# One output scale spread over all partitions by DMA through DRAM in place of TensorE, with reordered loads, shifts, banks and a split last tile

## What is computed

```python
mod = (silu(c) @ wmod).reshape(4, 6, 1, 512)
sa, ca, ga, sb, cb, gb = (mod[:, i] for i in range(6))
ga = sign(ga) * max(abs(ga), 0.25)              # gb likewise
h = layernorm(x) * (1 + ca) + sa
x = x + ga * attention(h, Wqkv, bqkv, Wo, bo)   # one head of 128
h = layernorm(x) * (1 + cb) + sb
x = x + gb * (h @ W_up.T + lora_of_top1_expert(h))
```

## Time and profile before

| | before |
|---|---|
| three runs, us | 184.07, 186.6, 189.16 (median 186.6) |
| the profiled execution, us | 184.51 |
| its span, first to last instruction, us | 182.8 |
| granted TensorE clock over the span | 1.000 (the level of 2.4 GHz) |
| busy share: PE, DVE, ACT, POOL | 93%, 76%, 49%, 44% |

### The profile page before, as it was taken

The page is one execution under the profiler, slowest core; times in us unless marked ns, Lnnn a source line. Parts: engine busy times, 40 slices in busy tenths (PEclk is TensorE's granted clock), DMA queues, the critical chain, the costliest instruction groups (busy, mean ns, idle before and its releaser), DMA issues.

```text
span 182.8 us, 2810 instructions
## 1 busy us (share of the span) xinstructions
PE 170.1 (93%) x911; PEld 133.6 (73%) x911; DVE 139.8 (76%) x350; ACT 90.3 (49%) x170; POOL 81.0 (44%) x109
## 2 busy tenths in 40 slices
PE   6778999999999959998999999999999999999990
PEld 6654756978678738786888787868887878768870
DVE  1837859997969999869997919699288294988964
ACT  3356145964268874176438552713396512484100
POOL 3464200279335984008769830018695000362650
PEclk9999999999999999999999999999999999999999
DMA  4999995930051014440023741001140000001414
GB/s 155 381 385 387 390 383 98 375 120 11 0 166 69 2 26 105 102 170 6 32 83 136 190 107 31 0 0 57 61 152 24 0 2 0 0 0 61 172 43 186
DMA packets 13758, 21.32 MB, mean 117 GB/s; under 512 B 3324, under 2 KB 3840, under 8 KB 13744
## 3 DMA queue, kind: packets, MB, share of 16 engines
q1 hardware_dynamic: 13744, 21.15, 34.3%
HBM read 14.83 MB, written 4.21 MB: 104 GB/s over the span
## 4 chain that ended last, share of the span: by engine, by line
PE 65%; DVE 18%; ACT 6%; DMA 4%; issue 4%; SPq 1%; POOL 0%; DVEq 0%; ACTq 0%; POOLq 0%
PE bank L391 43%; DMA stage<-in_L_wmod_dram 4%; PE bank L405 3%; DVE h1lo L1137 3%; PE bank L515 3%; DVE xs L1215 2%; DVE stats L1222 2%; PE bank L542 2%; DVE row_max L1189 2%; ACT xn_p L830 2%; DVE f_gb L1280 2%; DVE h2lo L1153 1%; DVE xn L1148 1%; PE bank L494 1%; PE bank L500 1%
## 5 line engine op out<-in xcount | busy, mean ns | idle before, releaser
L391 PE MATMUL bank<-wup_lo,h2hi 128*128 128x512 f32 x64 | 26.8, 418 | 1.3 <-DVE f_gb L1280 0.9
L1466 POOL TENSOR_TENSOR rstd<-var_eps,neg_half 128x1 f32<-128x1 f32 x16 | 8.8, 553 | 41.4 <-DVE var_eps L1226 41.4
L869 ACT ACTIVATE xn_p<-xs,shift,rstd 128x512 f32<-128x512 f32 x16 | 13.1, 817 | 25.9 <-POOL shift L1469 25.9
L391 PE MATMUL bank<-wup_hi,h2hi 128*128 128x512 f32 x64 | 25.3, 395 | 0.0
L391 PE MATMUL bank<-wup_hi,h2lo 128*128 128x512 f32 x64 | 25.2, 394 | 0.0
L1481 POOL TENSOR_TENSOR xs<-xs,f_gb 128x512 f32<-128x512 f32 x14 | 17.9, 1294 | 7.7 <-DVE f_gb L1280 7.7
L391 PE MATMUL bank<-h1lo,wqkv_hi 128*128 128x512 f32 x48 | 19.7, 410 | 0.8 <-DVE modT_ca L1057 0.8
L1458 POOL TENSOR_TENSOR xs<-xs,gabo 128x512 f32<-128x512 f32 x16 | 20.2, 1293 | 0.1
L391 PE MATMUL bank<-h1hi,wqkv_hi 128*128 128x512 f32 x48 | 19.0, 395 | 0.0
L391 PE MATMUL bank<-h1hi,wqkv_lo 128*128 128x512 f32 x48 | 18.9, 394 | 0.0
L391 PEld LDWEIGHTS bank<-wup_lo,h2hi 128*128 128x128 f32 x64 | 12.0, 188 | 4.5 <-DVE f_gb L1280 1.8
(11 more groups left out here) (181 smaller groups left out, 414.5 us busy)
## 6 DMA issues: line engine op xcount, KB each, us to landing
out_dram<-xs SPq DMA_DIRECT2D x16, 256.0 KB, 2.0
stage<-in_L_wmod_dram SPq DMA_DIRECT2D x3, 1024.0 KB, 8.0
xs<-in_L_wmod_dram SPq DMA_DIRECT2D x3, 1024.0 KB, 10.1
xs<-in_L_attn_x_dram SPq DMA_DIRECT2D x3, 1024.0 KB, 8.3
stage<-xn SPq DMA_DIRECT2D x32, 64.0 KB, 2.0
xs<-in_L_attn_x_dram SPq DMA_DIRECT2D x2, 512.0 KB, 3.9
f_gb<-in_L_ffn_W_up_dram SPq DMA_DIRECT2D x1, 1024.0 KB, 11.1
gb_bc<-gates_dram SPq DMA_DIRECT2D x4, 256.0 KB, 3.7
```

The source lines that it names most:

```text
L391: mm = nc.tensor.matmul(dst, w, m, start=first and i == 0, stop=last and i == total - 1)
L869: nc.scalar.activation(xn2_p[:, t, :], xs[:, b, t, :], ACT.Identity, bias=shift[:, 1, t:t + 1], scale=rstd[:, 1, t:t + 1]).then_inc(S["xn2 ...
L1466: nc.gpsimd.tensor_tensor(rstd[:, 1, t:t + 1], var_eps[:, 1, t:t + 1], neg_half[:, 0:1], ALU.pow).then_inc(S["ln2_rstd"], 1)
```

## The change

Batch 0's `ga` is no longer made by PE: `first_gate_everywhere`, its bank, its copy on ACT and two semaphores go. SP issues `spread_gate(0, 0)` after `write_gate(0)`, and the wait for the write moves from `write_gate` into `spread_gate`. DVE copies the gate rows after two of the four `pt_low` instead of after all. The rest of the change:

- Loads: `x` of batch 0 comes in three DMAs instead of two, and SP waits for the second before it issues two blocks of `wqkv`, and for the third before the section `sa`.
- DVE normalises tile 3 of batch 0 before it copies the first modulation rows; PE transposes that tile before it makes the columns of them.
- In batch 1, `gate_shift` and `gate_columns("gb")` come ahead of `v_low` and `turn_blocks(2)` on DVE, and the statistics of batch 3 after `o_low`. On ACT, `wo_high(1)` and half of `ln1_normalise(2)` move behind `gz_evacuate(0)`.
- `move_turned(2)` is cut in two halves on SP, with `write_gate(1)` between them.
- Banks: tile 3 of the FFN goes to another bank in batches 0 and 1, and so does the first third of the next `qkv`.
- The last tile of the last batch is computed, scaled, added and stored in two halves of 256 columns.

```diff
-        (1, "S", 0, 0), ... (6, "modT", 2), (6, "ga_bc"), (5, "gate_row", "ga"),
+        (1, "S", 0, 0), ... (6, "modT", 2), (5, "gate_row", "ga"),
-        order += [(m[i], "Y", b, t) for t, i in enumerate((1, 2, 3, 0))] + [(f[0], "F", b - 1, 3)]
+        order += [(m[i], "Y", b, t) for t, i in enumerate((1, 2, 3, 0))] + [(f[0] if last else m[4], "F", b - 1, 3)]
-            order += [(m[i], "qkv", b + 1, j) for j, i in enumerate((4, 1, 2))]
+            order += [(f[0], "qkv", b + 1, 0), (m[1], "qkv", b + 1, 1), (m[2], "qkv", b + 1, 2)]
...
             def write_gate(i):
                 sp.wait_ge(S["gates_ready"], i + 1)
                 sp.dma_start(gates_dram[i], gates[:, i, :]).then_inc(gates_out, 16)
-                sp.wait_ge(gates_out, 16 * (i + 1))
 
             def spread_gate(i, b):
+                sp.wait_ge(gates_out, 16 * (i + 1))
...
             load_section("ca")
+            sp.wait_ge(x0_in[1], 16)
             load_wqkv((0, 1))
+            sp.wait_ge(x0_in[2], 16)
             load_section("sa")
...
             write_gate(0)
+            spread_gate(0, 0)
             spread_gate(0, 1)
...
-            move_turned(2)
+            move_turned(2, (0, 1))
             write_gate(1)
+            move_turned(2, (2, 3))
...
             first_x1_transposes((2,))
+            first_x1_transposes((3,))
             first_modulation_columns(0)
             first_modulation_columns(1)
-            first_x1_transposes((3,))
...
             p_transposes(0, (0, 1, 2))
-            first_gate_everywhere()
             gate_to_rows("ga")
...
-            up(b, 3, (0, 1))
             z_transposes(b, 1)
-            up(b, 3, (2,))
+            for side in range(2):
+                last_tile_side(side, (0, 1, 2))
             lora_up(b, 2)
-            up(b, 3, (3,))
-            lora_up(b, 3)
+            for side in range(2):
+                last_tile_side(side, (3,))
...
-            pt_high(0, (0, 1, 2))
-            act.wait_ge(S["ga_bc_psum"], 1)
-            nc.scalar.activation(ga_bc[:, 0, :], at("ga_bc")[:], ACT.Copy).then_inc(S["ga_bc_ready"], 1)
-            pt_high(0, (3,))
+            pt_high(0)
...
-            wo_high(1)
-            ln1_normalise(2)
+            ln1_normalise(2, (0, 1))
             for b in range(1, B):
                 last = b == LAST
                 softmax(b, (0, 1, 2))
                 v_evacuate(b)
                 softmax(b, (3,))
                 gz_evacuate(b - 1)
+                if b == 1:
+                    wo_high(1)
+                    ln1_normalise(2, (2, 3))
...
-            first_modulation_rows()
             first_ln1_normalise()
+            first_modulation_rows()
...
-            pt_low(0)
+            pt_low(0, (0, 1))
             gate_rows_evacuate("ga")
+            pt_low(0, (2, 3))
...
             def output_weights(b):
+                pool.wait_ge(ga_bc_in[b % 2], 16 * (b // 2 + 1))
                 if b == 0:
-                    pool.wait_ge(S["ga_bc_ready"], 1)
```

The new function on PE for the last tile, and the end of DVE's program:

```diff
+            def last_tile_side(side, kts):
+                q, n = slice((NT - 1) * P, T), columns_of(side)
+                whole = open_bank("side", side) if kts[0] == 0 else at("side", side)
+                dst = whole[:, n]
+                products(dst, [((h2hi[:, kt, q], h2lo[:, kt, q]), (wup_hi[:, kt, n], wup_lo[:, kt, n])) for kt in kts],
+                         first=kts[0] == 0, last=False)
+                if kts[-1] == NK - 1:
+                    nc.tensor.matmul(dst, zT[:, q], lbw[:, n], start=False, stop=True).then_inc(S["F_psum"], 1)
...
+            for side in range(2):
+                part = columns_of(side)
+                dve.wait_ge(S["F_psum"], n + side + 1)
+                nc.vector.tensor_tensor(f_gb[:, n % 4, part], at("side", side)[:, part], gb_bc[:, LAST % 2, part],
+                                        ALU.mult).then_inc(S["f_gb_ready"], 1)
```

More of the change, by code:

```diff
@@ L198, in adaln_block @@
         wqkv_in = [sem(f"wqkv_in{kt}") for kt in range(NK)]
-        x0_in = [sem(f"x0_in{i}") for i in range(2)]
+        x0_in = [sem(f"x0_in{i}") for i in range(3)]
         x_in = [sem(f"x_in{b}") for b in range(B)]
@@ L265, in by_tokens, with columns_of @@
             return columns.rearrange("p (t c i) -> p c t i", c=NB, t=NT)
+        def columns_of(side):
+            return slice(side * H // 2, (side + 1) * H // 2)
         def xn1_done(engine, b, t=NT):
@@ L309, in spread_gate, with move_turned @@
                 sp.dma_start(to[:, b % 2, :], gates_dram[i, b].partition_broadcast(P)).then_inc(ready[b % 2], 16)
-            def move_turned(b):
-                sp.wait_ge(S["xn1_turned"], NT * (b - TURNED + 1))
-                if b > TURNED:
-                    sp.wait_ge(S["h1_lo"], NK * b)
-                for a in range(NB):
+            def move_turned(b, blocks=range(NB)):
+                if blocks[0] == 0:
+                    sp.wait_ge(S["xn1_turned"], NT * (b - TURNED + 1))
+                    if b > TURNED:
+                        sp.wait_ge(S["h1_lo"], NK * b)
+                for a in blocks:
                     for c in range(NB):
@@ L362, in _ @@
                     move_turned(3)
-                for t in range(NT):
-                    if b == LAST and t >= 2:
-                        sp.wait_ge(last_out_ready, t - 1)
-                    else:
-                        sp.wait_ge(S["out_ready"], NT * b + t + 1)
+                for t in range(NT if b < LAST else 2):
+                    sp.wait_ge(S["out_ready"], NT * b + t + 1)
                     sp.dma_start(out_v[b, :, t, :], xs[:, b, t, :]).then_inc(stored, 16)
@@ L429, in gate_to_rows @@
                 mm.then_inc(S["gate_row_psum"], 1)
-            def first_gate_everywhere():
-                dst = open_bank("ga_bc")
-                pe.wait_ge(S["gate_col_ready"], 1)
-                for kt in range(NK):
-                    mm = nc.tensor.matmul(dst[:, kt * P:(kt + 1) * P], gate_col[:, 0, kt, 0:1].to_broadcast([P, P]), ident[:],
-                                          start=True, stop=True)
-                mm.then_inc(S["ga_bc_psum"], 1)
             def qkv_shift_rows():
@@ L846, in o_high, with ln1_normalise @@
                 nc.scalar.activation(o_hi[:], at("O", b)[:], ACT.Copy).then_inc(S["o_hi_ready"], 1)
-            def ln1_normalise(b):
-                for t in range(NT):
+            def ln1_normalise(b, tiles=range(NT)):
+                for t in tiles:
                     act.wait_ge(S["ln1_shift"], BY_ACT + NT * (b - 2) + t + 1)
@@ L1403, in _ @@
             gate_ffn(LAST, 1)
-            for t in (2, 3):
-                gate_ffn(LAST, t)
-                n = NT * LAST + t
-                dve.wait_ge(S["f_gb_ready"], n + 1)
-                nc.vector.tensor_tensor(xs[:, LAST, t, :], xs[:, LAST, t, :], f_gb[:, n % 4, :],
+            gate_ffn(LAST, 2)
+            n = NT * B - 2
+            dve.wait_ge(S["f_gb_ready"], n + 1)
+            nc.vector.tensor_tensor(xs[:, LAST, 2, :], xs[:, LAST, 2, :], f_gb[:, n % 4, :],
+                                    ALU.add).then_inc(last_out_ready, 1)
+            n = NT * B - 1
+            dve.wait_ge(S["out_ready"], n - 3)
+            for side in range(2):
+                part = columns_of(side)
+                dve.wait_ge(S["F_psum"], n + side + 1)
+                nc.vector.tensor_tensor(f_gb[:, n % 4, part], at("side", side)[:, part], gb_bc[:, LAST % 2, part],
+                                        ALU.mult).then_inc(S["f_gb_ready"], 1)
+                dve.wait_ge(S["f_gb_ready"], n + side + 1)
+                nc.vector.tensor_tensor(xs[:, LAST, 3, part], xs[:, LAST, 3, part], f_gb[:, n % 4, part],
                                         ALU.add).then_inc(last_out_ready, 1)
```

36 lines of the change are left out of this document (19 added, 17 removed), and 2 rows, old and new, of the table order.

## The result

The changed kernel takes 189.2 us (median of four runs, 187.87 to 190.67), where 186.4 was forecast: just past the upper end of the range, 189.2. The kernel before had a median of 185.3 us beside it (four runs, 183.73 to 189.16). The kernel before has fast executions near 184.5 us and slow ones near 189.5 (32 of its 52 in the later comparisons took 188.9 to 191.6), and every ratio here compares fast executions with fast ones, so that it can differ from the ratio of the medians. The ratio is 1.028, with a 95% interval of 1.022 to 1.034: slower, by some 5 us, where the sum of the prediction had 0.8. Those 32 have a mean granted clock of 0.968 to 0.982: in most of its executions the kernel before pays for a lower clock already, and its median over all 52, 189.3 us, is that of the changed kernel.

The account below looks back on a forecast made before the run. PE, busy 93% of the span, was taken as the bound. Terms +3.1 (stall), -2.3 (gate bias), +0.2 (banks), +0.1 (start), -0.3 (end) gave +0.8 us on 185.6: 186.4 us, range 183.6 to 189.2.

Parts of the forecast that it names:

- the rival: PE idle some 3 us in the `W_up` transposes halves its clock, adding 1.5 to 2 us: about 188.2; chance 0.08.
- the stall: In the `W_up` transposes PE waits for DVE's `h1_low(1)`, held back by ACT's `wo_hi` and late ga: +3.1 us.
- taking ga off PE: Before `pv(0)` in batch 0, 1.0 us taken from PE becomes 1.0 us more waiting on DVE: gain 0.
- the gate bias: In batch 1, an earlier `gz_bias` on DVE removes PE's wait for the expert gate: gain 2.3 us.
- the block moves: Batch 1's 16 moves on SP end at 80.6, so `h1_high(2)` starts at 80.65 instead of 79.97, in before's clock.
- banks and what is late next: Batches 1 and 2: bank gains 0.7 and 0.3, losses 0.2, 0.8 and 0.2; together a loss of 0.2 us.
- `qkv(2)`: It opens the bank that `f_gb` empties, at 86.5 against PE there at 86.3: loss 0.2 us.
- `qk_lo`: In `scores(2)` the third matmul needs both parts, which DVE ends at 97.9: loss 0.8 us.
- the maxima and the expert gate: After `scores(2)`, they run 1.2 us ahead where PE is 2.0 ahead: loss 0.2 us.
- the start: Before PE's first real work, tile 3's order costs 0.3 us and held loads gain 0.2: loss 0.1 us.
- the end: Last tile in two halves, with a last store of 128 KB instead of 256 KB: gain 0.3 us, between 0 and 0.6.

Follow-up runs that it names:

- the DMA way alone: The kernel before with only batch 0's ga made by DMA, DVE copying the gate rows after two `pt_low`: 191.99 us, ratio 1.034.
- one spread: The changed kernel with the second spread of ga issued after the load of batch 3's x: 188.40 us, ratio 1.021.
- the other moves alone: The changed kernel with batch 0's ga made by TensorE again, the rest of the change kept: 182.54 us, ratio 0.991.
- the kernel with 14 products: The changed kernel with 14 unused identity products on PE between blocks 1 and 2 of the `W_up` transposes: 187.83 us, ratio 1.018.
- the kernel at 182.17: The changed kernel with TensorE's ga back, tile 3's old order and SP's waits ahead of `wqkv` undone: 182.17 us, ratio 0.988.

## Why the prediction was wrong

**Wrong: the chance and the price of the clock.** The sum had no term for it. The step that failed is in the rival: the wait of 2.27 us that "left the granted clock at 1.00" was taken as a case of waits in general, and the chance set to 0.08. One wait in one execution was too thin for that. A wait of 2.26 us at the same place was followed by the halved clock in another execution of nearly the same kernel. The changed kernel's four runs all had a clock of 0.991 or less, the DMA way alone 0.991 or less in four, one spread 0.990 or less in four; the other moves alone 0.995 or more in four. In profiles, stalls of 3.3, 4.0 and 4.1 us here were each followed by the fall, and with the stall filled by PE the clock stayed at 1.00. Its price was set at 1.5 to 2 us, for 3 to 4 us of work at the lower level; PE worked for 6 us at it, and 2.8 us were lost. The row that could have warned stood in view: three runs of one kernel 5 us apart are more than the profile of the fastest explains. The prediction took the middle, 185.6, as the kernel's level; of 52 later executions two lay between 185.3 and 188.8. The rule of the Trainium skill, page "TensorE: Matmul & The Clock Gate", section "What's actually happening", was named in the rival, and set aside against one row; it says the clock follows how busy the array has been, and the windows above agree with it.

**Nearly right: the stall.** Predicted 3.1 us, measured 3.5 on PE (an idle 3.27 us by the row). The place, the releaser and each link hold. Taking off the 0.5 us of the later start, the spread was issued at 37.7 (37.9 forecast) and POOL began at 41.2 (41.0): 3.5 us from issue to use instead of 3.1. Behind `wo_ga` the chain took 3.3 us, as forecast. The write had been placed between two ends by when the last section of `wmod` landed; it took 1.6 us here and 2.5 with one spread.

**Right: nothing gained by taking ga off PE.** The forecast moved its 1.0 us into the wait before `pv(0)`, and that wait is 1.18 us, for `plo`, where it is 0.18 with TensorE's passes. Against the profile before, 0.11 us were gained.

**Right: the gate bias**, -2.3 forecast and -2.43 measured. `h1_high(2)` starts 7.24 us later than before, where PE was 6.73 late by then: the block moves slipped by 0.5 where 0.7 was forecast.

**Right in the sum, banks and what is late next:** +0.2 forecast, +0.13 measured. That is luck in part, since the terms missed by up to 0.3 each way. The losses were 0.5 instead of 0.2 for `qkv(2)`, 0.65 instead of 0.8 for `qk_lo`, and 0.22 in `out_projection(1)`, which was not forecast; of the 0.2 for the maxima and the expert gate at most 0.1 came. The gains were 0.74 for 0.7, and 0.60 for 0.3.

**Too small: the start.** +0.1 forecast, +0.5 measured: the order costs 0.4 rather than 0.3, and the held loads brought no earlier landing (PE starts on the section 0.13 later). The section landed 7.70 us after its issue instead of 7.96, but SP issued it 0.39 later, at 2.58 instead of 2.19, behind the three loads of `x` that were two; the sum had no term for that.

**Wrong by little: the end.** -0.3 forecast, 0 measured. DVE's last half ends 4.73 us later than before, 0.3 more than PE's offset, because four halves of 0.42 take longer than two passes of 0.69; the smaller last store gives that back.

The sum with measured sizes: 0.53 - 0.11 + 3.48 + 2.83 - 2.43 + 0.13 + 0 = +4.4. Of the miss of 3.6, 2.8 are the clock, 0.4 the stall, 0.4 the start, 0.3 the end, less 0.3 in the smaller terms.

## What to carry to other kernels

A new wait on a TensorE that is nearly always busy has two prices: its length, and what the clock takes behind it (here 3.5 and 2.8 us). Ask for the second at every wait of the order of two or three microseconds, and look in the single runs, not only in the profiled one, for a spread that a fall would explain: the profile of the fastest execution can show a wait at no price that costs 5 us in most of the others. Work moved from the bound engine to a DMA round trip pays only if that engine doesn't then wait for another, and if nothing of its own stands behind the operation that waits for the landing: here ACT, in its order, made two blocks of `h1` wait for a scale that they don't use.

## What was not expected

The same idleness of PE gives different clocks: 2.0 us at the start kept it at 1.00 in the changed kernel, 2.1 and 2.3 us at the same place halved it in two others, and even 3.0 us there kept it in the kernel with 14 products, as 2.85 did in the kernel at 182.17; 2.26 us in batch 1 kept it in one execution and halved it in another. A write of 8 KB to DRAM and its semaphore took 1.4 to 3.3 us in these profiles, and from the issue of the 256 KB read behind it to its user's start lay 3.1 to 4.0 us (from 37.57 to 41.60 in the DMA way alone). And a single late stretch put three of VectorE's four `h1lo` beside GpSimd's work, where one had been: 2.1 us more for the four.
